# Logits of the first attention from float32r high and low parts, made by GpSimd

## What is computed

```
Q = einsum('bmd,hdk->bhmk', x, P_q)
K = einsum('bmd,hdk->bhmk', x, P_k)
V = einsum('bmd,hdv->bhmv', x, P_v)
logits = einsum('bhmk,bhnk->bhmn', Q, K) * 8, causal mask
key_weights = softmax(logits)
o = einsum('bhmm,bhmv->bhmv', key_weights, V)    # only the diagonal weight of each token
x = layernorm(x + einsum('bhmv,hdv->bmd', o, P_o))
```

## Time and profile before

| | |
|---|---|
| time, median of 3 runs | 3484.22 us (3483.04 to 3484.29) |
| the profiled execution: its own time | 3485.04 us |
| the profiled execution: its span | 3483.2 us |
| busy share of the whole span | PE 98%, ACT 88%, DVE 86%, POOL 72% |
| first attention | from 0 to about 443 us of the span |
| granted TensorE clock in the windows of this stage | 1.00 of full speed |

### The profile page before, as it was taken

One profiled execution on the slowest core, in us unless ns is written; L12 is line 12 of the kernel. 1 busy time (PEld: TensorE's weight loads), 2 busy tenths in 40 slices (PEclk: granted clock), 3 DMA queues, 4 the chain that ended last, 5 costly groups with the idle time before them and its releaser, 6 DMA issues. The chain is left out here.

```text
span 3483.2 us, 177745 instructions
## 1 busy us (share of the span) xinstructions
PE 3410.3 (98%) x70388; PEld 2881.8 (83%) x70388; DVE 2991.3 (86%) x7016; ACT 3056.1 (88%) x10549; POOL 2494.3 (72%) x2057
## 2 busy tenths in 40 slices
PE   8999999999999999999999999999999999999998
PEld 5666677888888888888888888888888888888877
DVE  8999988888888888888888888888888888888886
ACT  8999978898988888888888888888888889888886
POOL 0121178887878878788787887878888788887874
PEclk9999999999999999999999999999999999999999
DMA  2000011111211111121111121111211111111111
GB/s 105 8 5 20 5 53 53 48 42 43 57 55 50 44 44 46 54 57 48 46 44 50 52 57 47 43 42 54 59 48 46 43 47 54 45 46 47 51 42 44
DMA packets 177474, 160.59 MB, mean 46 GB/s; under 512 B 113933, under 2 KB 124813, under 8 KB 176397
## 3 DMA queue, kind: packets, MB, share of 16 engines
q1 hardware_dynamic: 176653, 149.22, 15.2%
HBM read 25.71 MB, written 4.19 MB: 9 GB/s over the span
## 5 line engine op out<-in xcount | busy, mean ns | idle before, releaser
L1544 POOL TENSOR_TENSOR a_rn<-a_ssqc,a_minus_half 128x16 f32<-128x16 f32 x384 | 1113.4, 2900 | 256.3 <-DVE a_ssqc L1751 252.1
L1428 ACT ACTIVATE late<-bank,a_negmax 128x64 f32<-128x64 f32 x3072 | 963.9, 343 | 31.0 <-DVE a_negmax L1705 29.4
L1562 POOL TENSOR_TENSOR a_r<-a_u,a_rn 128x512 f32<-128x512 f32 x768 | 800.7, 1043 | 55.9 <-DVE a_u L1733 10.5
L1428 ACT ACTIVATION_READ_ACCUMULATOR late<-bank,a_negmax 128x1 f32 x3072 | 728.6, 237 | 0.0
L1717 DVE TENSOR_TENSOR a_u<-bank,a_rot_c 128x512 f32<-128x512 f32 x768 | 524.7, 683 | 175.3 <-ACT a_sq L1404 174.7
L1551 POOL TENSOR_TENSOR a_PN<-late,a_erec 128x256 f32<-128x256 f32 x768 | 487.9, 636 | 255.8 <-DVE a_erec L1758 241.4
L1726 DVE TENSOR_TENSOR a_v<-bank,a_rot_s 128x512 f32<-128x512 f32 x768 | 522.7, 681 | 0.0
L1733 DVE TENSOR_TENSOR a_u<-a_u,a_v 128x1024 f32<-128x1024 f32 x384 | 469.7, 1223 | 25.6
L1404 ACT ACTIVATE a_sq<-bank 128x512 f32<-128x512 f32 x768 | 462.8, 647 | 17.2 <-PE bank L1013 16.7
L1411 ACT ACTIVATE a_QK<-bank 128x512 f32<-128x512 f32 x768 | 465.8, 607 | 4.1 <-PE bank L1054 1.9
L1054 PE MATMUL bank<-ident,a_r 128*128 128x128 f32 x3072 | 463.3, 274 | 5.2 <-ACT late L1396 1.8
(11 more groups left out here) (190 smaller groups left out, 7757.2 us busy)
## 6 DMA issues: line engine op xcount, KB each, us to landing
a_V_sh<-a_V_nat SPq DMA_DIRECT2D x384, 192.0 KB, 2.5
a_V_sh<-a_V_nat SPq DMA_DIRECT2D x192, 64.0 KB, 2.4
late<-in_qkv SPq DMA_DIRECT2D x20, 384.0 KB, 3.7
a_x_sh<-X SPq DMA_DIRECT2D x48, 128.0 KB
a_V_sh<-a_V_nat SPq DMA_DIRECT2D x192, 32.0 KB, 2.1
a_x_sh<-X SPq DMA_DIRECT2D x48, 127.0 KB
late<-X SPq DMA_DIRECT2D x47, 128.0 KB
late<-X SPq DMA_DIRECT2D x47, 127.0 KB
```

Of the source, the lines that this page charges most:

```text
L1428: ins = act.activation(E[:, s.par, k, :], scores[:, hp, col:col + KW], ACT.Exp, bias=negmax[:, s.par, k:k + 1], accum_out=esum[:, s.par, k ...
L1544: pool.tensor_tensor(rn[:, a.par, :], ssqc[:, a.par, :], minus_half[:, :], ALU.pow).then_inc(S["rn"], 1)
L1562: pool.tensor_tensor(heads(r[:, a.par, half]), heads(u[:, a.par, half]), rn[:, a.par, mm * 2 * HG:(mm + 1) * 2 * HG].unsqueeze(2).to_broad ...
```

## The change

ACT now copies the projection to a two-part buffer `qk_sb`. POOL makes from it the high part `QKh` (a copy that rounds to float32r) and the low part `QKl` (the subtraction). PE forms the logits in three float32r terms, each issued for both heads before the next: high by high, high by low, low by high. `F_LOGITS` goes from 2 to 3 and `F_DIAGONAL` from 4 to 5. To make room in SBUF, the buffer of the raw qkv weights now lies on that of the projection weights, and its load waits until the last of them has been split (`w_lo` 6).

```
-F_X, F_LOGITS, F_DIAGONAL = 12, 2, 4
+F_X, F_LOGITS, F_DIAGONAL = 12, 3, 5
...
-        QK = sb("QK", [P, 3, 2, T])
+        qk_sb = sb("qk_sb", [P, 2, T])
+        QKh, QKl = sb("QKh", [P, 3, 2, T], F32R), sb("QKl", [P, 3, 2, T], F32R)
...
+                sp.wait_ge(w_lo, 6)
+                sp.dma_start(raw[:, :, :], dram["qkv"][0]).then_inc(S["weights"], 16)
...
-                                pe.wait_ge(y_out, s.k - s.pos % 2 + 2)
+                                pe.wait_ge(qk_lo, s.k - s.pos % 2 + 2)
...
-                            for h, (_, i, n) in enumerate(both):
-                                side, q, w = slice(DH * h, DH * h + DH), slice(i * P, (i + 1) * P), (i + 1) * P
-                                pe.matmul(p_s[n % F_BANKS][:, 0:w], QK[side, pair, 0, q], QK[side, pair, 1, 0:w],
-                                          start=True, stop=True)
+                            for term, (query, key) in enumerate(((QKh, QKh), (QKh, QKl), (QKl, QKh))):
+                                for h, (_, i, n) in enumerate(both):
+                                    side, q, w = slice(DH * h, DH * h + DH), slice(i * P, (i + 1) * P), (i + 1) * P
+                                    pe.matmul(p_s[n % F_BANKS][:, 0:w], query[side, pair, 0, q], key[side, pair, 1, 0:w],
+                                              start=(term == 0), stop=(term == 2), skip_group_check=True)
...
-                            ge(act, logits_ready, 2 * (a.k - part - 4))
-                            act.activation(QK[:, pair, part, :], p_y[:, :], ACT.Copy, scale=1.0 if part else 8.0).then_inc(y_out, 1)
+                            ge(act, qk_lo, a.k - 1)
+                            act.activation(qk_sb[:, part, :], p_y[:, :], ACT.Copy, scale=1.0 if part else 8.0).then_inc(y_out, 1)
...
-                    o, before = at(b, j, STEPS), at(b, j, 3 * STEPS)
+                    a, o, before = at(b, j, 0), at(b, j, STEPS), at(b, j, 3 * STEPS)
+                    if a:
+                        pair, part = (a.k // 2) % 3, a.pos % 2
+                        pool.wait_ge(y_out, a.k + 1)
+                        ge(pool, logits_ready, 2 * (a.k - part - 4))
+                        pool.tensor_copy(QKh[:, pair, part, :], qk_sb[:, part, :]).then_inc(qk_hi, 1)
+                        pool.wait_ge(qk_hi, a.k + 1)
+                        pool.tensor_tensor(QKl[:, pair, part, :], qk_sb[:, part, :], QKh[:, pair, part, :].bitcast(F32),
+                                           ALU.subtract).then_inc(qk_lo, 1)
```

More of the change, by code:

```diff
@@ L114, in first_attention @@
         sem = lambda name: ctx.enter_context(nc.semaphore("f_" + name))
-        pw = [sb(n, [P, H * DH]) for n in ("pq_sb", "pk_sb", "pv_sb")]
+        pw_sb = sb("pw_sb", [P, 3 * H * DH])
+        pw, raw = [pw_sb[:, i * H * DH:(i + 1) * H * DH] for i in range(3)], pw_sb.rearrange("p (g c) -> p g c", g=G)
         wh = [sb(n, [P, H * DH], F32R) for n in ("pqh", "pkh", "pvh")]
@@ L131, in first_attention @@
         masks_f = sb("masks_f", [P, 2, 4 * KW])
-        raw = sb("raw", [P, G, 3 * CQ])
         st, ag = sb("st", [P, MT, 6]), sb("ag", [P, MT, 2])
@@ L141, in first_attention @@
         xh_ready, xl_ready = sem("xh_ready"), sem("xl_ready")
-        y_ready, y_out = (sem(n) for n in ("y_ready", "y_out"))
+        y_ready, y_out, qk_hi, qk_lo = (sem(n) for n in ("y_ready", "y_out", "qk_hi", "qk_lo"))
         logits_ready, max_ready, exp_ready = (sem(n) for n in ("logits_ready", "max_ready", "exp_ready"))
@@ L185, in _ @@
                 for dst, src in w.up_loads(dram, 0) + (w.down_load(dram, 0),) + (
-                        (raw[:, :, :], dram["qkv"][0]), (w.scales[:, :, :], dram["scales"][0].partition_broadcast(P)),
+                        (w.scales[:, :, :], dram["scales"][0].partition_broadcast(P)),
                         (w.out[:, :, :], dram["wo"][0]), (A["tabs_c"][:, :, :, :], dram["rot_cos"]),
@@ L315, in projected @@
                         if a:
-                            pair, part = (a.k // 2) % 3, a.pos % 2
+                            part = a.pos % 2
                             act.wait_ge(y_ready, a.k + 1)
-                            ge(act, logits_ready, 2 * (a.k - part - 4))
-                            act.activation(QK[:, pair, part, :], p_y[:, :], ACT.Copy, scale=1.0 if part else 8.0).then_inc(y_out, 1)
+                            ge(act, qk_lo, a.k - 1)
+                            act.activation(qk_sb[:, part, :], p_y[:, :], ACT.Copy, scale=1.0 if part else 8.0).then_inc(y_out, 1)
                     def exps(turn):
```

## The result

The changed kernel takes 3553.79 us (median of 5 runs, 3546.16 to 3556.30) against 3484.22 us before: a ratio of 1.0195, 95% interval 1.018 to 1.021. It is 70 us slower; 38 were forecast.

What follows compares the result with a forecast made beforehand. PE sets the pace, DVE close behind; DVE's waits for POOL's SBUF reads make DVE the pace. 72 positions give +10, 56 with `f_O` +22, filling +4, `all_ready` +2: +38 us, 3522; likeliest range 3500 to 3565, whole 3475 to 3595.

Steps and rivals of the forecast that it cites:

- The Trainium skill's rule: DVE instructions with two SBUF inputs and POOL instructions reading SBUF exclude each other for the whole instruction.
- if DVE gets in between, it waits as before, 3.53. I take the middle, 3.79: Positions with `f_O`: 4.05 us if DVE waits through all POOL's work, 3.53 if not; middle 3.79, giving +22 us.
- the 3.08 us of DVE's own work: DVE's work in a mean position without its present losses, 3.24 - 9.0 / 59 = 3.08 us.
- rival 1: Broken groups: waiting POOL operations get between a group's four diagonals; 3560 to 3600 us, at most +214; chance 0.11.
- The second estimate: 0.31 us lost per 1.04 us product; POOL's new work costs 69, less 19 spare, plus 6 for the ends: 3540 us.
- the 19 us that DVE has to spare: DVE's spare time in the first stage, 128 positions x 0.15 us; relief of PE alone can bring no more.
- POOL's prices: Each position's copy taken as 0.78 us and subtraction as 1.04, together 1.82, or 2.86 with `f_O`.
- PE's gain: Three float32r logit terms save PE 0.40 us a position, or about 0.15 if narrow matmuls cost as much as 512-column ones.
- rival 2: POOL's work falls beside DVE's maxima, so DVE does not wait: -19 us and +4 for filling, 3469 us; chance 0.18.
- The lags and the filling: First maxima one projection later plus POOL's 1.82, +4 us; later `all_ready` at 7 batches, +2; qkv load, nothing.

Runs made afterwards that it cites:

- pool_alone: Kernel before, float32 logits and its lags, plus POOL's copy and subtraction into buffers that nothing reads: 3550.43 us, ratio 1.0189.
- reduce_after: Changed kernel with each diagonal operation replaced by a sum with one SBUF input: 3488.71 us, against 3483.95 us for the same edit on the kernel before.
- bank_after: Changed kernel with diagonals taken from the logits in the bank ahead of each maximum, weights formed once a batch: 3487.02 us, ratio 1.0003.
- gated: Changed kernel with POOL one position later and its copy held until DVE has finished the position's diagonals: 3529.73 us, ratio 1.0126.
- memsets: Kernel before plus POOL's work alone, with two memsets a position in place of its copy and subtraction: 3505.79 us, ratio 1.0057.
- terms_alone: Changed kernel's three terms and lags 3 and 5 without POOL's work, ACT writing the high part, low parts zero: 3476.98 us, ratio 0.9973.

## Why the prediction was right, and what was mis-sized

**Direction and mechanism: right.** POOL's reads hold DVE's operations of two SBUF inputs, DVE becomes the pace, the layers don't change. Shown by `pool_alone` (+65 us without anybody using the parts), `reduce_after` (+5 us with all of POOL's work), `bank_after` (the same operation with one input in a bank, never over 293 ns), and the diagonals' durations. The Trainium skill's rule (SBUF, "Who interferes with whom") is borne out here for two-input operations against reads of 512 columns; there it also says that a GpSimd operation that only writes leaves them alone, and the diagonal at 227.85 beside the memset agrees.

**The size: 70 us, not 38.** The step that failed is "if DVE gets in between, it waits as before, 3.53. I take the middle, 3.79": it let a group of diagonals wait once, at its first member. A second one is the 3.08 us of DVE's own work in the 3.53: it is a mean over both kinds of positions. The timeline of the changed kernel shows what a group can do when POOL's queue is full:

```profile
227.18 1.28 POOL L389 TENSOR_TENSOR f_QKl<-f_qk_sb,f_QKh 128x512 fp32r<-128x512 f32 x1
...
227.23 1.38 DVE L455 SCALAR_TENSOR_TENSOR f_diag_only<-f_E,ident 128x128 f32<-128x128 f32 x1
...
228.42 1.09 POOL L398 TENSOR_TENSOR f_O<-late 128x512 f32<-128x512 f32 x1
...
228.54 1.12 DVE L455 SCALAR_TENSOR_TENSOR f_diag_only<-f_E,ident 128x128 f32<-128x128 f32 x1
...
229.50 0.63 POOL L387 CAST f_QKh<-f_qk_sb 128x512 fp32r<-128x512 f32 x1
...
229.59 0.68 DVE L455 SCALAR_TENSOR_TENSOR f_diag_only<-f_E,ident 128x128 f32<-128x128 f32 x1
...
230.21 0.28 DVE L455 SCALAR_TENSOR_TENSOR f_diag_only<-f_E,ident 128x128 f32<-128x128 f32 x1
230.21 1.42 POOL L389 TENSOR_TENSOR f_QKl<-f_qk_sb,f_QKh 128x512 fp32r<-128x512 f32 x1
...
230.62 1.03 DVE L467 TENSOR_TENSOR f_prob<-f_ediag,f_erec 128x4 f32<-128x4 f32 x1
```

The first diagonal (227.23) waits for the subtraction, the second (228.54) for `f_O`, the third (229.59) for the next copy, and the product L467 (230.62) for the next subtraction. In this group DVE gets one operation done, once two, between two of POOL's. That is rival 1, which I priced apart with 0.11. It came true in part: of the 56 groups in positions with `f_O`, 24 have three or four members that wait over 0.15 us, 21 have one and 11 none. The time lies in the forecast's own range, 3500 to 3565, but with a piece of a rival in it that the forecast had left out; that much of the hit is luck.

Counted from DVE's own diagonals, in us a position from the second batch on:

| | position | DVE's waits | its own work | idle |
|---|---|---|---|---|
| with `f_O`, before | 3.22 | 0.34 | 2.80 | 0.08 |
| with `f_O`, changed | 4.02 | 1.19 | 2.79 | 0.04 |
| without, before | 3.53 | 0.02 | 3.22 | 0.29 |
| without, changed | 3.81 | 0.38 | 3.30 | 0.12 |

A wait is here what a diagonal takes above 0.28 us and a product above 0.164. With `f_O` the prediction took 0.71 us of waiting (3.79 - 3.08), at most 0.97; it is 1.19, and 0.27 of that is the product, a fifth member that my sum left out. Without `f_O` it took 0.45, and the waits are no longer than that, 0.38. There the position is longer than 3.53 because DVE's own work is 3.2 to 3.3 us and not 3.08: normalisations and the like fall into these positions, and what they add is missing in the others (2.8). By the evictions, 56 x (4.09 - 3.79) = 17 us and 72 x (3.74 - 3.53) = 15 us make up the 32 that I missed.

The second estimate, by the rate of loss per us of POOL's work, gave 3540. Its rate came out: 69 us of new waits forecast, 74 measured. What was too high in it is the 19 us that DVE has to spare, taken off in full: from the second batch on DVE's idle time falls only from 19 to 10 us, so 65 us are left, as the evictions show. The rate itself is no constant, though. It is the waits per us of POOL's 512-column reads, 0.34 in the kernel before, 0.30 in the changed one, 0.24 in `gated` and 0.86 in `memsets`: it depends on where the reads fall, and that it held here is luck.

**POOL's prices.** Copy 0.61 us (0.78 taken), subtraction 1.28 (1.04 taken): 1.89 where 1.82 was taken, +0.07 us a position. The product `f_O` was the wrong row for the subtraction.

**PE's gain: too high.** 0.40 us a position was worked out at the 512-column rate. The timeline of an even position:

```profile
227.78 0.33 PE L225 MATMUL bank<-f_QKh 64*128 64x128 f32 x2
...
227.94 0.27 PE L225 MATMUL bank<-f_QKl,f_QKh 64*128 64x128 f32 x2
...
228.06 0.28 PE L225 MATMUL bank<-f_QKh,f_QKl 64*128 64x128 f32 x2
...
228.17 0.23 PE L230 MATMUL bank<-f_mask_b,f_pick_b 64*128 64x64 bf16 x4
...
228.24 0.47 PE L225 MATMUL bank<-f_QKh 64*128 64x512 f32 x2
...
228.56 0.40 PE L225 MATMUL bank<-f_QKl,f_QKh 64*128 64x512 f32 x2
...
228.79 0.40 PE L225 MATMUL bank<-f_QKh,f_QKl 64*128 64x512 f32 x2
...
229.03 0.23 PE L230 MATMUL bank<-f_mask_b,f_pick_b 64*128 64x64 bf16 x4
```

From 227.78 to 229.03 it is 1.25 us, against 1.32 from 108.04 to 109.36, with the masks between the two pieces (0.07 and 0.06) in both. The three terms of 128 columns take 0.39 us, more than float32's 0.32; those of 512 take 0.79 against 0.94. That is neither 0.40 less nor four times the price for the narrow one. By the medians of the whole stage, an even position falls from 1.27 to 1.18 us and an odd one (256 and 384 columns) from 1.26 to 1.07 (in `terms_alone`), a gain of 0.14 us on the mean: this is the prediction's lower end of 0.15, though made up otherwise. The heads do run side by side. `terms_alone` shows what it is worth: 8.6 us where rival 2 had 15, with the 2.4 us of the lags in it. It changed nothing here, as the prediction said.

**The lags and the filling: right in size, as far as tested.** +4 (filling, 1.8 of it POOL's parts) and +2 forecast; the lags alone cost 2.4 us (within 0 to 5). The qkv load was not tried by itself; the runs with it (`reduce_after`, 5 us above its control) leave little room for a cost.

**Rival 2** (POOL's work beside the maxima) was tested by `gated`, which forces it: 24 us come back, and not all, since `f_O` still falls beside the diagonals and PE now waits for the parts. It doesn't happen by itself.

## What to carry to other kernels

Before work is given to an idle POOL, list DVE's operations with two inputs in SBUF: each of them and each of POOL's 512-column reads take turns. So the sum of both must fit into a position, and here, with `f_O`, it does not: 2.96 us of POOL (0.61, 1.28 and 1.07) and 1.0 of DVE in a position of 3.3. That it fits is not enough: without `f_O` it is 2.89 us, and the position still grew by 0.30, since the two fall together. When POOL has its next operation ready, several members of a group of such DVE operations can each wait for one of POOL's, so count members and not only groups. And take DVE's own work for each kind of position by itself. Where an input can stay in PSUM, or the operation has one input and is a reduction, POOL's room is real: the same 1.9 us a position then cost 5 us in all instead of 65.

## What was not expected of the hardware

- In the group shown above the two engines go by turns: of five DVE operations of two SBUF inputs, four waited, 1.1, 0.8, 0.4 and, after one free, 0.9 us, for four successive operations of POOL (227.2 to 231.6 us).
- Not every operation of POOL that reads holds them. The power operation on 128x4, L403 in `memsets`, lasts 1.11 us, and diagonals inside that time keep their 0.29 us (16 of them in the kernel before, none over 0.293). The rule that the prediction quotes, for the whole instruction, does not hold for this one:

```profile
228.10 1.11 POOL L403 TENSOR_TENSOR f_rstd<-f_ve,f_mhalf 128x4 f32<-128x4 f32 x1
...
228.27 0.29 DVE L454 SCALAR_TENSOR_TENSOR f_diag_only<-f_E,ident 128x128 f32<-128x128 f32 x1
```

- A memset of POOL (write only) leaves the two-input diagonals at 0.28 us, but a DVE normalisation L590 of one full SBUF input beside it took 0.87 us for a pair where 0.60 is usual.
- POOL's subtraction of two full 512-column inputs takes 1.28 us, with a float32r or a float32 result, and its copy 0.61; the product with a broadcast input takes 1.04 to 1.07.
- Two heads' float32r matmuls of 64 rows and 128 columns take 0.11 to 0.16 us a term, two to three times the 0.06 that a 512-column one of 0.23 us would give by its columns.
- The granted TensorE clock from 200 to 250 us was 0.97 of full speed on the mean. It was at the lower of its two levels (0.50, 1.2 GHz) for 3.4 us, and PE had been busy 7.88 of the 10 us before; in the kernel before PE was busy 9.93 of the same 10 us, and the clock stayed at 1.00 (2.4 GHz). The changed stage has eight such drops, 31 us in all, while PE had time to spare. The windows of 237.2 to 247.2 and 247.2 to 250.6 us in the changed kernel:

```profile
237.20:247.20 10.00, 7.88 (x71) 5.61 (x67) 9.90 (x43) 7.58 (x24) 3.78 (x4) 1.00 0.10 28
247.20:250.60 3.40, 3.40 (x12) 2.60 (x10) 3.29 (x18) 2.89 (x10) 1.89 (x2) 0.50 0.01 2
```
